# First part of a recurrent attention: gate sums stored chunk by chunk, query decays spread by DMA, first score moved ahead of batch 1's keys

## The reference, cut to what matters

```
logfg = log_sigmoid(f_pre); Fcum = cumsum(logfg)
Dmat  = Fcum[s] - Fcum[t] + i_pre[t]        (causal: t <= s)
m     = max_t Dmat;  Smat = exp(Dmat - m)
C     = (q k^T / sqrt(dqk)) * Smat
n     = max(|sum_t C|, exp(-m));  h = (C / n) v
```

## Time and profile before

| | |
|---|---|
| time, median of 3 runs | 697.85 us (697.79 to 698.93) |
| the profiled execution: its time | 698.43 us |
| its span | 696.5 us |
| PE busy | 669.8 us (96% of the span) |
| ACT busy | 372.0 us (53%) |
| DVE busy | 517.4 us (74%) |
| POOL busy | 131.1 us (19%) |

### The profile page before, as it was taken

How to read it: one execution, slowest core, us unless ns; L and a number is a source line. 1 busy time by engine, 2 the same in 40 slices (tenths; PEclk the granted TensorE clock), 3 DMA queues, 4 the chain that set the end, 5 groups by cost and what they waited for, 6 DMA issues and landing times.

```text
span 696.5 us, 12153 instructions
## 1 busy us (share of the span) xinstructions
PE 669.8 (96%) x4808; PEld 560.3 (80%) x4808; DVE 517.4 (74%) x919; ACT 372.0 (53%) x775; POOL 131.1 (19%) x125
## 2 busy tenths in 40 slices
PE   7998998999999999999999999999999999999996
PEld 7866775778787888878888878887777898889886
DVE  6736778887956576566675575757679998989996
ACT  5886878846644444344353442446666455364541
POOL 7144535410000020000200002000123213203220
PEclk9999999999999999999999999999999999999999
DMA  5099452000101001010001100150000000000000
GB/s 196 5 264 299 105 155 71 2 1 0 63 1 31 0 1 63 0 31 1 1 23 40 32 1 0 42 233 2 0 1 0 1 2 31 1 31 1 1 31 31
DMA packets 24008, 31.27 MB, mean 45 GB/s; under 512 B 1232, under 2 KB 19952, under 8 KB 23184
## 3 DMA queue, kind: packets, MB, share of 16 engines
q1 hardware_dynamic: 23296, 29.18, 13.6%
q10 hardware_dynamic: 656, 1.31, 0.5%
HBM read 28.18 MB, written 2.31 MB: 44 GB/s over the span
## 4 chain that ended last, share of the span: by engine, by line
PE 66%; DVE 23%; ACT 6%; issue 3%; POOL 1%; DMA 1%; DVEq 0%
PE bank L94 21%; PE bank L96 19%; PE bank L95 19%; DVE l_ring_lo L2544 3%; DVE l_ge L2525 2%; DVE l_h L2540 2%; DVE l_o L2548 1%; DVE h_raw L1220 1%; DVE l_h L2497 1%; ACT m_W L709 1%; PE bank L519 1%; DVE h_ring_lo L1225 1%; DVE m_st L938 1%; PE bank L507 1%; PE bank L492 1%
## 5 line engine op out<-in xcount | busy, mean ns | idle before, releaser
L1220 DVE TENSOR_TENSOR h_raw<-h_s,bank 128x512 f32<-128x512 f32 x104 | 71.4, 686 | 107.9 <-ACT h_s L1210 93.5
L1210 ACT ACTIVATE h_s<-bank 128x512 f32<-128x512 f32 x104 | 62.2, 598 | 164.1 <-PE bank L96 164.0
L1225 DVE TENSOR_TENSOR h_ring_lo<-h_raw,h_ring_hi 128x512 fp32r<-128x512 f32 x92 | 68.9, 749 | 0.1
L1214 ACT ACTIVATE h_ring_hi<-h_raw 128x512 fp32r<-128x512 f32 x104 | 64.7, 622 | 2.3 <-DVE h_raw L1220 2.3
L95 PE MATMUL bank<-fused_lo,h_ring_hi 128*128 128x256 f32 x208 | 58.4, 281 | 0.0
L2244 ACT ACTIVATE l_s<-bank 128x512 f32<-128x512 f32 x32 | 19.1, 598 | 62.7 <-PE bank L96 62.5
L94 PE MATMUL bank<-l_xT_hi,l_wgu 128*128 128x512 f32 x128 | 51.2, 400 | 0.3
L94 PE MATMUL bank<-f_yT_hi,mlp_hi 128*128 128x512 f32 x128 | 50.6, 396 | 0.2 <-DVE f_yT_lo L1333 0.2
L96 PE MATMUL bank<-l_xT_hi,l_lo 128*128 128x512 f32 x128 | 50.0, 391 | 0.0
L95 PE MATMUL bank<-l_xT_lo,l_wgu 128*128 128x512 f32 x128 | 50.0, 390 | 0.0
L96 PE MATMUL bank<-f_yT_hi,fused_lo 128*128 128x512 f32 x128 | 50.0, 390 | 0.0
(11 more groups left out here) (372 smaller groups left out, 1972.8 us busy)
## 6 DMA issues: line engine op xcount, KB each, us to landing
m_W<-m_scratch SPq DMA_DIRECT2D x16, 512.0 KB, 6.8
fused_raw<-in_fused SPq DMA_DIRECT2D x1, 3584.0 KB, 12.9
res<-in_x SPq DMA_DIRECT2D x4, 512.0 KB, 6.1
fused_raw<-in_fused SPq DMA_DIRECT2D x2, 1024.0 KB, 9.3
f_mask<-expert_weights SPq DMA_DIRECT2D x8, 256.0 KB
l_raw<-in_layer SPq DMA_DIRECT2D x1, 2048.0 KB, 8.7
out_x<-res SPq DMA_DIRECT2D x16, 128.0 KB, 1.9
f_xw<-in_turned_x SPq DMA_DIRECT2D x3, 512.0 KB, 5.5
```

The lines of the kernel that those rows point to most:

```text
L1210: self.nc.scalar.activation(self.s[u % 2][r, :], gate[r, :], ACT.Silu).then_inc(self.silu.sem, 1)
L1214: self.nc.scalar.activation(self.unit(i, u)[0], self.product(i, u), ACT.Copy).then_inc(self.hi.sem, 1)
L1220: self.nc.vector.tensor_tensor(out=self.product(i, u), in0=self.s[u % 2][r, :], in1=up[r, :], op=ALU.mult).then_inc(self.hidden.sem, 1)
L1225: self.nc.vector.tensor_tensor(out=lo, in0=self.product(i, u), in1=f32(hi), op=ALU.subtract).then_inc(self.lo.sem, 1)
```

## The change

The gate sums are stored to DRAM as (chunk, row, position) in place of (row, position), so that the 8 rows of one chunk lie in one piece of 4 KB; the load then names rows of 1024 floats in place of 8 x 128. `qrow` is stored to DRAM too, and four DMAs spread it to `eq`, one a batch, placed in SP's list between the loads of W0 to W4, with the same semaphore as W1 to W4 (`landed(n)` counts both, so POOL's mask of W1 to W4 waits for both, and ACT's `decay_of_queries(b)` waits for the decay rows of batch b and for W of n = b+1). PE's four decay products go. ACT's exponentials of the decays now read and write `eq` in SBUF, and all four stand behind `weights(0)`. `score(0)` stands ahead of `project_k(1)`. DVE does `weigh_scores(0)` ahead of `weigh_q(0)`. The rest of the diff writes `gated_sum` as its two parts and splits `if b:` blocks, with the same instructions in the same order.

```diff
-    scratch = nc.dram_tensor("m_scratch", (R, S), fp32, kind="Internal").ap()
+    scratch = nc.dram_tensor("m_scratch", (C, R, P), fp32, kind="Internal").ap()
...
+    landed = lambda n: 16 * (n // RING + 1 + (1 <= n % RING <= B))
+    decay_rows = nc.dram_tensor("m_decay_rows", (R, S - P), fp32, kind="Internal").ap()
...
-            rows = scratch[of(b), chunk(c)].unsqueeze(0).to_broadcast([P, H, P])
-            sp.dma_start(W[n % RING][:, :, :], rows).then_inc(loaded[n % RING], 16)
+            rows = scratch[c, of(b), :].rearrange("h s -> (h s)").unsqueeze(0).to_broadcast([P, H * P])
+            sp.dma_start(W[n % RING][:, :, :].rearrange("p h s -> p (h s)"), rows).then_inc(loaded[n % RING], 16)
 
         sp.wait_ge(dve_rows, G_ROW)
-        sp.dma_start(scratch, row[5][0:R, :]).then_inc(stored, 16)
+        sp.dma_start(scratch.rearrange("c r s -> r c s"), row[5][0:R, :].rearrange("r (c s) -> r c s", s=P)).then_inc(stored, 16)
+        sp.wait_ge(dve_rows, Q_ROW)
+        sp.dma_start(decay_rows, qrow[:, :]).then_inc(rows_of_decay, 16)
         sp.wait_ge(stored, 16)
         sp.wait_ge(gated, 1)
-        for n in range(RING):
+        spread_rows(0)
+        sp.wait_ge(rows_of_decay, DECAY_STORED)
+        for n in range(1, RING):
+            if n <= B:
+                rows = decay_rows[of(n - 1), :].unsqueeze(1).to_broadcast([H, DQ, S - P])
+                sp.dma_start(eq[:, n - 1, :], rows).then_inc(loaded[n], 16)
             spread_rows(n)
...
-            for b in range(B - 1):
-                spread_decay(b)
-
-        def spread_decay(b):
-            if b == B - 1:
-                pe.wait_ge(eq_ready.sem, eq_ready.at(b - 1, 1))
-            nc.tensor.matmul(spread_banks[b][:, 0:S - P], head_spread[:, b, :], qrow[:, :], start=True, stop=True).then_inc(tables_t, 1)
...
             else:
-                pe.wait_ge(eq_ready.sem, eq_ready.at(1, 1))
                 pe.wait_ge(act_tables, ENDS_IN)
...
-        project_k(1)
         pe.wait_ge(dve_tables, GA)
         pe.wait_ge(splitting.low, splitting.all)
         score(0)
-        spread_decay(B - 1)
+        project_k(1)
         project_q(1)
...
         def decay_of_queries(b):
-            act.wait_ge(tables_t, SPREAD_T + b)
-            nc.scalar.activation(eq[:, b, :], spread_banks[b][:, 0:S - P], ACT.Exp, scale=-1.0).then_inc(eq_ready.sem, 1)
+            act.wait_ge(loaded[b + 1], landed(b + 1))
+            nc.scalar.activation(eq[:, b, :], eq[:, b, :], ACT.Exp, scale=-1.0).then_inc(eq_ready.sem, 1)
...
-        decay_of_queries(0)
-        decay_of_queries(1)
         act.wait_ge(dve_tables, GA)
         nc.scalar.activation(ea[:, 0, :, :], ga[:, :, :], ACT.Exp).then_inc(act_tables, 1)
-        decay_of_queries(2)
         weights(0)
-        decay_of_queries(3)
         copy_k(1)
+        decay_of_queries(0)
         weights(1)
         copy_q(1)
+        for b in range(1, B):
+            decay_of_queries(b)
...
-            pool.wait_ge(loaded[n % RING], 16 * (n // RING + 1))
+            pool.wait_ge(loaded[n % RING], landed(n))
...
+        weigh_scores(0)
         weigh_q(0)
-        weigh_scores(0)
```

More of the change, by code:

```diff
@@ L303, in mlstm_phase @@
     Y1, SLACK, SOFT0, SOFT1, F_SUM, A_ROW, G_ROW, Q_ROW, M_ROW, DIAG = range(1, 11)
-    TG_T, ENDS_T, SPREAD_T = range(1, 4)
+    TG_T, ENDS_T = range(1, 3)
     TG_IN, ENDS_IN, EA_M, DEXP, EA_K = range(1, 6)
@@ L307, in mlstm_phase @@
     DEC, GA = range(1, 3)
+    landed = lambda n: 16 * (n // RING + 1 + (1 <= n % RING <= B))
     IDENT_READY, CONSTANTS = 3, 28
+    decay_rows = nc.dram_tensor("m_decay_rows", (R, S - P), fp32, kind="Internal").ap()
+    rows_of_decay, DECAY_STORED = cols_loaded, 48
     eq_ready, loaded = sg("m_eq", 1), [one(f"m_W_loaded{n}") for n in range(RING)]
@@ L323, in mlstm_phase @@
     turn_banks = [[bank[0], bank[1]], [bank[2], bank[3]]]
-    tg_bank, small_bank, spread_banks = bank[0], bank[1], [bank[2], bank[3], bank[4], bank[4]]
+    tg_bank, small_bank = bank[0], bank[1]
     ends_cols = slice(B * C, B * C + C * R)
@@ L369, in _ @@
             sp.dma_start(g.x_rows[1, b].rearrange("(c s) -> c s", s=P), x_rows[2 * b * C:(2 * b + 1) * C, 1, :]).then_inc(stored, 16)
-        sp.wait_ge(tables_t, SPREAD_T + B - 1)
+        sp.wait_ge(tables_t, ENDS_T)
         sp.wait_ge(og_t.sem, og_t.at(0, 2))
@@ L514, in weighted @@
                 pe.wait_ge(evicted.sem, evicted.at(b, 2 * c))
-            else:
-                pe.wait_ge(eq_ready.sem, eq_ready.at(B - 1, 1))
             for h in range(H):
@@ L604, in _ @@
                 project_k(b + 1)
+            if b:
                 project_q(b + 1)
@@ L1000, in mean_square @@
             nc.vector.tensor_reduce(out=den[f][3][:, x], in_=sq[:, some, :].rearrange("p c (h d) -> p (c h) d", d=DV), op=ALU.add, axis=AX.X).then_inc(ms_steps.sem, 1)
-        def gated_sum(b, f):
-            sum_squares(b, f)
-            gate(b, f)
         def sum_squares(b, f):
@@ L1107, in _ @@
                 mean_square(b - 1, 1)
+            if b:
                 add(b - 1, 0)
-                gated_sum(b - 1, 1)
+            if b:
+                sum_squares(b - 1, 1)
+            if b:
+                gate(b - 1, 1)
             weigh_q(b + 1)
@@ L1121, in _ @@
                 add(b - 1, 1)
-            gated_sum(b, 0)
+            sum_squares(b, 0)
+            gate(b, 0)
             weigh_scores(n + 3)
@@ L1145, in _ @@
         mean_square(b, 1)
-        gated_sum(b, 1)
+        sum_squares(b, 1)
+        gate(b, 1)
         following.split_low(dve, 0, 1)
@@ L1150, in _ @@
         mean_square(b, 2)
-        gated_sum(b, 2)
+        sum_squares(b, 2)
+        gate(b, 2)
         low_h(b, 0)
```

## The result

The changed kernel takes 703.51 us (median of 4 runs, 702.59 to 704.21), the kernel before 698.16 us on the same chip (4 runs, 697.79 to 698.93). The ratio is 1.0071, with a 95% interval of 1.0058 to 1.0084: 5.3 us slower. The profiled execution took 703.46 us with a span of 701.6 us, against 698.43 and 696.5. The prediction was 699.7 us with a range of 696.8 to 702.8, so the time lies above the range.

What follows compares the result with a forecast made beforehand. The prediction took the start of ACT's `weights(2)` to bound the kernel: 1.5 us later there plus 0.4 us for PE's clock gave +1.9 us on 697.85, forecast 699.7 us, range 696.8 to 702.8.

Steps and rivals of the forecast that it cites:

- What bounds the kernel: ACT's start of `weights(2)`, 47.57 us before, decides; its shift moves PE's values at 54.57 and all behind one to one.
- W0's load: SP's load of W0 in 4 KB rows: 4.8 us from issue to landing, 5.1 before; `weights(0)` starts 0.3 us earlier.
- The W loads behind it: Four W loads behind W0 run at the full rate, 4 x 1.34 = 5.36 us, in the sum landing at 48.2.
- The decay loads: Four decay loads run on half of the DMA engines, holding up W loads queued there: 4 x 1.06 = 4.24 us.
- ACT's order: Four decays in ACT's busy row: 8.30 us to `weights(2)`, which also waits behind the last decay; in all 1.5 us late.
- D: Rival: the shared DRAM region slows every load, `weights(2)` at 50.9 to 55.1, +3.3 to +7.6 us; chance 0.15.
- PE's clock: PE idles some 3.6 us before the keys and its clock falls to 0.50: 0.4 us taken, bounds 0 and 1.7.
- No cost for PE's products and the score's order: On PE, dropping four decay products is worth at most 0.20 us; `score(0)` ahead of `project_k(1)` costs 0.
- A: The forecast itself: ACT waits for W4 and the last decay rows before `weights(2)`, +0.9 to +2.9 us; chance 0.43.

Runs made afterwards that it cites:

- e1: The kernel before with only the gate sums stored chunk by chunk and W loaded in 4 KB rows, decays staying products; 696.35 us, ratio 0.9976.
- e12: The changed kernel without its four decay loads, POOL zeroing the decay rows instead, all orders kept; 697.66 us, ratio 0.9985.
- e10: e1 with three more 512 KB loads between W0 and W1, all 128 partitions reading one 4 KB row; 702.28 us, one run.
- e2: The changed kernel with every decay row stored twice, so the decay loads' source has slowest dimension 16, not 8; 701.47 us, ratio 1.0046.
- e9: e1 with three more 512 KB loads between W0 and W1, each partition reading its own 4 KB row; 700.52 us, one run.
- e3: The changed kernel with the decays of batches 2 and 3 moved later in ACT's list, to where their batch needs them; 699.95 us, ratio 1.0022.
- e8: The kernel before with `score(0)` ahead of `project_k(1)` on PE and nothing else; 698.76 us, ratio 0.9999.
- e5: e1 with 16 copies of the gate-sum rows stored, so W1 to W3 read 16 regions, not one shared; 699.35 us, one run.
- e4: The changed kernel with 20 useless matmuls on PE behind chunk 0's weighted product; 701.31 us, ratio 1.0049.
- e11: The changed kernel with the changes of e2 and e3 and 13 useless matmuls on PE together; 698.34 us, ratio 0.9994.
- e6: e3 with 13 useless matmuls on PE behind chunk 0's weighted product; 700.07 us, ratio 1.0015.

## Why the prediction was wrong, step by step

**What bounds the kernel** held. The start of `weights(2)` decided the place of the values on PE, and that moved the end nearly one to one (5.90 us at the values, 5.1 at the end; 1.63 and 2.2 us earlier in e1). What follows can shift that by a microsecond: e12 is 0.24 us late at the values and 0.9 early at the end.

**W0's load** was mis-sized the other way: 3.8 us from issue to landing, not 4.8. "I take 4.8, since all engines reading one 4 KB region is what the change keeps" rested on `f_x_rows`, and e10 shows 128 partitions reading one row of 4 KB at 414 GB/s, so the shared region isn't what slows such a load. The same load took 3.4 us (e12), 3.5 (e1), 4.0 (e2), 4.2 (e9) and 4.7 (e10) in other executions. This made the forecast too late by a microsecond here, and hid part of the next miss.

**The W loads behind it** are the step that failed: "four W at the full rate 4 x 1.34 = 5.36 (the two halves are apart by then, and read different regions)". In e1, without any decay load, the four took 8.8 us from landing to landing. The term is 3.5 us too small. With W0's microsecond the other way, 0.15 us more for the decay loads and an issue 0.1 us later it makes the 2.7 us by which the landing, 50.9, missed the predicted 48.2. The row to use was on hand: the earlier trace rows has W0's mask at 38.96 and W4's at 47.61, 2.2 us a load. The prediction set that aside, because the issues took 10.28 us and seemed to be what spaced the loads; e1 cuts them to 3.37 us and the spacing stays. As the price of such a load the term was sound, since W1 to W4 land 1.2 us apart in e9 and e10; as the price in this stretch, right behind W0, it was not.

**The decay loads** were right in mechanism and size: 4 x 1.06 = 4.24 us against 4.4 measured, on half of the engines, as e2 confirms by nearly halving them and as W5's counts show in the changed kernel itself. By the rule of the Trainium skill's page "DMA: Bandwidth & Descriptors" (Why a DMA increments its semaphore by 16 and not by 1, on how many engines) a slowest dimension of 16 reaches all the engines. The 2.4 us of e2 agree with it. The formula of the same page of the Trainium skill (Anatomy of one DMA) is fitted to DMAs that GpSimd issues, which the prediction left out; W0 is issued by SP. Its estimate of 3.2 us for W0 lies 0.6 us under the 3.8 measured; the 4.8 that the sum took lies 1.0 over.

**ACT's order.** That `weights(2)` waits behind the last decay was right, and e3 undoes it. The busy row without waits was predicted at 8.30 us, and e12 shows 8.45. The waits for the decays of batches 0 and 2 and for W1 (0.59, 0.74 and 0.72 us) weren't predicted, but they only took time that the last wait would have filled. Waits ahead of the second decay and of `weights(1)` were the sign that the prediction gave for D; they came, from loads that were slow for another reason.

**PE's clock** was right in mechanism and too small: 0.4 taken, 1.62 measured, near the bound of 1.7. The wait of 1.04 us before the values was counted as cover for most of it; it is still 0.75 us behind the fall, so only 0.3 us of it was used. The chain of work that ended last says why: these microseconds are ACT's copy of values that PE had finished only at 59.7. The price is no constant: 0.93 us in e12, 1.62 here, 2.28 in e3, each by the distance from `weights(2)` to the values less the 7.00 of before.

**No cost for PE's products and the score's order** was right for the order (e8); the products alone were not tried.

Of the rivals, D gave the size (701.2 to 705.4) but its cause is wrong by e5 and e10; A gave the mechanism. The sum by measured terms is 4.28 for `weights(2)`, 1.62 for the clock, less 0.65 taken up later: 5.25 us, against 5.1 by the spans and 5.3 by the medians; the 0.35 us that came back at 120 us is not in it, nor are small shifts behind that place.

**Open:** why W1 to W4 take 2.2 us each in e1 and 1.2 us each in e9 and e10. Neither region, broadcast nor time explains it, and e5, e9 and e10 are one execution each.

## What to carry to other kernels

Take the price of a load in a stream from the distance between the landings of that same stream, not from a plain load elsewhere, whatever seems to explain the distance; and as the same loads can run at half or at full rate, give such a term a range. In an engine's list, data needed later isn't waited for ahead of work needed now: moving two waits gave back two thirds of the loss. A broadcast over partitions should have 16 in its slowest dimension (e2), and an idle TensorE costs its wait once and its low clock behind it again.

## What the runs showed of the hardware

- TensorE's granted clock stood at 0.50 behind waits of 5.18 us, 3.14 us (e3) and 2.29 us (e12), and over 44 to 46 us in the changed kernel, behind a wait of 1.99 us. It stood at 1.00 behind 1.90 us with useless matmuls ahead of it (e4).
- Six broadcast loads of 512 KB take 3.37 us to issue with 4 KB rows and 10.28 us with 512-byte rows, and land at nearly the same distance.
- A stream of DMA loads with all engines busy (share 1.0 or more) moves 228 to 450 GB/s, by stretches of some microseconds, in one and the same kernel (e1: 228 over 38 to 42, 450 over 42 to 46, where plain loads of the next phase are among them).
- Four 192 KB loads whose source has 8 in its slowest dimension hold up what is queued behind them on half of the engines: in the changed kernel W5 is through on eight engines at 47.79 us and reaches the other eight from 50.49 on.
- One DMA engine can finish a load 0.9 to 1.7 us behind the fifteen others: W4 in e1 (1.35), W2 in e2 (1.68), W1 in e10 (1.31). Each time a fetch of 16 KB of instructions had begun 2.5 to 3.6 us before that last count, at 43.14, 42.51 and 42.79; that it is the cause is not shown.
- The four `xn` pieces on DVE take 1.37 us alone and longer when a mask of POOL lies over them. In the kernel before the timeline of DVE, then that of POOL, has them together:

```profile
63.65 2.03 DVE L1046 TENSOR_SCALAR xn<-res,moment,roots 128x256 f32<-128x256 f32 x4
```

```profile
63.47 1.09 POOL L847 TENSOR_SCALAR_AFFINE_SELECT m_W<-m_W 128x1024 f32<-128x1024 f32 x1
```

In the changed kernel the mask starts at 67.11, is over at 68.20, and DVE's row stands clear of it:

```profile
69.56 1.37 DVE L1043 TENSOR_SCALAR xn<-res,moment,roots 128x256 f32<-128x256 f32 x4
```

Over these kernels the price goes with the overlap: none costs nothing (e1, e12, and here), 0.67 us of it 0.40 (e11), 0.91 us 0.66 (before), 1.15 us 0.80 (e6) and 1.00 (e8). So 0.65 us of e1's gain of 2.2 goes with where a mask happens to fall, which no forecast here took in; no run moved that mask alone.
